# Edge blocks of a graph network: segment sums in bf16 over rows split into three parts by VectorE

## The reference

```python
def _ln(x, g, b): ...                        # layer norm over 64 features
def _mlp(x, w0, b0, w1, b1):
    return jax.nn.silu(x @ w0 + b0) @ w1 + b1
...
for s in range(S):                           # S = 2 blocks
    ce = jnp.concatenate([e, n[senders], n[receivers]], axis=-1)
    e = e + _ln(_mlp(ce, edge_blk_w0[s], edge_blk_b0[s], edge_blk_w1[s], edge_blk_b1[s]), ...)
    agg = jax.ops.segment_sum(e.astype(jnp.float32), receivers, num_segments=num_nodes)
    cn = jnp.concatenate([n, agg.astype(n.dtype)], axis=-1)
    n = n + _ln(_mlp(cn, node_blk_w0[s], ...), ...)
return _mlp(n, dec_w0, dec_b0, dec_w1, dec_b1)
```

## Time and profile before

| | us |
|---|---|
| median of 3 runs | 22607.06 (22599.68 to 22610.77) |
| the profiled execution's own time | 22640.54 |
| its span, first to last instruction | 22638.8 |
| POOL busy | 11698.9 |
| PE busy | 13646.0 |
| DVE busy | 9714.0 |
| ACT busy | 2931.8 |
| indirect DMAs of s0 and s1 (L804), issue time | 6148.6 |

### The profile page before, as it was taken

The page is one execution under the profiler, slowest core; times in us unless marked ns, Lnnn a source line. Parts: engine busy times, 40 slices in busy tenths (PEclk is TensorE's granted clock), DMA queues, the critical chain, the costliest instruction groups (busy, mean ns, idle before and its releaser), DMA issues. The chain is left out here.

```text
span 22638.8 us, 317898 instructions
## 1 busy us (share of the span) xinstructions
PE 13646.0 (60%) x88696; PEld 10718.9 (47%) x88696; DVE 9714.0 (43%) x29825; ACT 2931.8 (13%) x5120; POOL 11698.9 (52%) x12296
## 2 busy tenths in 40 slices
PE   2555555554787777845655555555456666666664
PEld 1444444443677677734444444444334444444443
DVE  4333333333666666643333333333343333333333
ACT  0222222221000000011111111111111111111111
POOL 5656565565444444444444444444445555555553
PEclk7666666565899899966666666666666666666666
DMA  2111111112111001113333333333323333333331
GB/s 86 54 55 55 55 55 54 56 54 58 20 21 21 20 20 21 21 44 102 102 101 102 102 101 102 102 102 101 88 78 93 92 93 92 93 92 93 91 92 53
DMA packets 1995040, 1603.29 MB, mean 71 GB/s; under 512 B 1291419, under 2 KB 1461007, under 8 KB 1994047
## 3 DMA queue, kind: packets, MB, share of 16 engines
q10 hardware_dynamic: 939256, 906.14, 12.2%
q0 software_dynamic: 394560, 282.16, 6.6%
q1 hardware_dynamic: 661104, 413.62, 6.5%
HBM read 990.92 MB, written 612.64 MB: 71 GB/s over the span
## 5 line engine op out<-in xcount | busy, mean ns | idle before, releaser
L804 POOL DMA_INDIRECT s_gt<-ta_d,s_ix x6448 | 6148.6, 954 | 5990.0 <-DVE s_ix L857 3804.4
L804 POOL DMA_INDIRECT g_gt<-xs_d,g_ix x3224 | 3047.6, 945 | 2084.4 <-DVE g_ix L857 1069.4
L1001 PE MATMUL pair<-g_part,g_Oh 128*128 128x224 bf16 x25389 | 2994.4, 276 | 750.9 <-issue 723.6
L1001 PEld LDWEIGHTS pair<-g_part,g_Oh 128*128 128x128 bf16 x25389 | 2531.5, 104 | 1123.4 <-issue 1001.4
L804 POOL DMA_INDIRECT g_gt<-ys_d,g_ix x2015 | 1921.1, 953 | 2124.8 <-DVE g_ix L857 1509.5
L1048 PEld LDWEIGHTS psw<-s_R,s_P 128*128 128x128 f32 x12896 | 2016.7, 228 | 2071.3 <-issue 2045.3
L1048 PE MATMUL psw<-s_R,s_P 128*128 128x64 f32 x12896 | 2001.9, 303 | 1421.6 <-issue 1392.9
L1015 PE MATMUL pair<-e_w,s_hT 128*128 128x128 f32 x6448 | 1350.9, 376 | 2240.6 <-ACT s_hT L953 1652.8
L1048 PE MATMUL psw<-g_R,g_P 128*128 128x80 f32 x6448 | 1250.3, 374 | 1831.2 <-ACT g_sg L958 1775.7
L1015 PEld LDWEIGHTS pair<-e_w,s_hT 128*128 128x128 f32 x6448 | 1195.0, 277 | 2385.4 <-ACT s_hT L953 1369.0
L1048 PEld LDWEIGHTS psw<-g_R,g_P 128*128 128x128 f32 x6448 | 1178.6, 282 | 2289.4 <-issue 2267.1
(11 more groups left out here) (329 smaller groups left out, 15662.6 us busy)
## 6 DMA issues: line engine op xcount, KB each, us to landing
s_dl<-dl_d SPq DMA_DIRECT2D x404, 512.0 KB
seg_d<-s_sg ACTq DMA_DIRECT2D x806, 256.0 KB
seg_d<-g_sg ACTq DMA_DIRECT2D x403, 320.0 KB
z_d<-g_rT ACTq DMA_DIRECT2D x403, 256.0 KB
s_z<-z_d ACTq DMA_DIRECT2D x403, 256.0 KB
s_gt<-ta_d,s_ix POOLq DMA_INDIRECT x6448
s_Bw<-tb_d ACTq DMA_DIRECT2D x3224, 32.0 KB
s_Bw<-tb_d SPq DMA_DIRECT2D x3224, 32.0 KB
```

Source lines behind the costliest of these rows:

```text
L804: eng.indirect_dma_start(out=gt[k][:, s, :], out_offset=None, in_=table[:, :], in_offset=bass.IndirectOffsetOnAxis(ap=ix[k][:, s:s + 1], a ...
L1001: last = eng.matmul(near_out(k, t), Oh[k][:, g, 128 * t:128 * t + 128], part[n][:, g, :, :].rearrange("p f l -> p (f l)"), start=g == 0 an ...
```

## The change

In s0 and s1 (and, as before, in g2) `cut` is now true. The one-hot `P` is bf16, and after writing the rows `R` DVE cuts them into three bf16 parts `Rp` whose sum is exactly the float32 value. PE's segment sums then take 24 bf16 matmuls (8 groups x 3 parts, accumulated in float32) where s0 and s1 had 8 float32 ones. DVE's scratch for the remainder is the square buffer `sq` of the same tile. A new semaphore, `v_cut`, says that the parts are there: PE waits for it before the segment sums, ACT before it overwrites `sq` two tiles later. In g2 the same four operations stay with another layout of `Rp`. The bias tables are three pieces of one tile at partitions 0, 32 and 64.

```diff
+        e_b1s = sbuf(ctx, "e_b1s", [67, 512], BF16)
+        e_b1 = [e_b1s[32 * i:32 * i + 3, :] for i in range(3)]
+        ones67 = sbuf(ctx, "ones67", [67, 128], BF16)
+        ones3 = ones67[0:3, :]
...
-                thin = near and not mlp
-                P = many("P", [128, G, 128], BF16 if thin else F32)
+                cut = expand or near and not mlp
+                P = many("P", [128, G, 128], BF16 if cut else F32)
+                if cut:
+                    Rp = many("Rp", [128, 3, G, FS], BF16)
...
+                if cut:
+                    rest = sq if mlp else many("rest", [128, G, FS])
...
+                    def parts_of(eng, k):
+
+                        eng.drain()
+                        eng.tensor_copy(Rp[k][:, 0, :, :], R[k][:, :, :])
+                        eng.drain()
+                        eng.tensor_tensor(rest[k][:, :, :], R[k][:, :, :], Rp[k][:, 0, :, :], ALU.subtract)
+                        eng.drain()
+                        eng.tensor_copy(Rp[k][:, 1, :, :], rest[k][:, :, :])
+                        eng.drain()
+                        return eng.tensor_tensor(Rp[k][:, 2, :, :], rest[k][:, :, :], Rp[k][:, 1, :, :], ALU.subtract)
...
                                 eng.tensor_tensor(R[k][:, :, 0:64], ps[2 + k][:, :].rearrange("p (s f) -> p s f", s=G),
                                                   bc(yy[:, :].rearrange("p (s o) -> p s o", o=1), [128, G, 64]),
                                                   ALU.mult).then_inc(v_ln.sem, 1)
+                                if cut:
+                                    parts_of(eng, k).then_inc(v_cut.sem, 1)
...
-                            done(eng, v_ln, j, L_LN + 2)
+                            done(eng, v_cut if cut else v_ln, j, L_LN + 2)
...
-                            eng.matmul(ps[2 + k][:, :], ones3[:, :], mlp[1][:, :], start=False, stop=True,
+                            eng.matmul(ps[2 + k][:, :], ones67[32 * mlp[1]:32 * mlp[1] + 3, :], e_b1[mlp[1]], start=False, stop=True,
...
+                            if cut:
+                                done(eng, v_cut, j, L_SEG)
...
-                                for n in range(3 if thin else 1):
-                                    last = eng.matmul(psw[:, SP_ * t:SP_ * t + FS], P[k][:, s, :], Rp[k][:, s, n, :] if thin else R[k][:, s, :],
-                                                      start=n == 0, stop=n == 2 or not thin)
+                                for n in range(3 if cut else 1):
+                                    last = eng.matmul(psw[:, SP_ * t:SP_ * t + FS], P[k][:, s, :], Rp[k][:, n, s, :] if cut else R[k][:, s, :],
+                                                      start=n == 0, stop=n == 2 or not cut)
```

More of the change, by code:

```diff
@@ L112, in build @@
         e_w1 = [sbuf(ctx, f"e_w1_{i}", [128, 128]) for i in range(3)]
-        e_b1 = [sbuf(ctx, f"e_b1_{i}", [3, 512], BF16) for i in range(3)]
-        ones3 = sbuf(ctx, "ones3", [3, 128], BF16)
+        e_b1s = sbuf(ctx, "e_b1s", [67, 512], BF16)
+        e_b1 = [e_b1s[32 * i:32 * i + 3, :] for i in range(3)]
+        ones67 = sbuf(ctx, "ones67", [67, 128], BF16)
+        ones3 = ones67[0:3, :]
         e_w0 = sbuf(ctx, "e_w0", [16, 128])
@@ L294, in dve @@
                     eng.memset(ones[:, :], 1.0)
-                    eng.memset(ones3[:, :], 1.0)
+                    eng.memset(ones67[:, :], 1.0)
                     eng.memset(one2[:, :], 1.0)
@@ L691, in build @@
         v_pt, p_rt, a_rt, v_sum, a_zr = [mark(f"e_{n}") for n in ("vpt", "prt", "art", "vsum", "azr")]
-        p_u, v_red, v_tab = [mark(f"e_{n}") for n in ("pu", "vred", "vtab")]
+        p_u, v_red, v_tab, v_cut = [mark(f"e_{n}") for n in ("pu", "vred", "vtab", "vcut")]
         s_m = [ctx.enter_context(nc.semaphore(f"e_mark{b}")) for b in range(2)]
@@ L737, in edge_loop @@
                     own = sbuf(c, f"{tag}_sel", [128, xp, FG, GL])
-                    Rp = many("Rp", [128, G, 3, FG], BF16)
-                    rest = sbuf(c, f"{tag}_rest", [128, G, FG])
                 if zout is not None:
@@ L891, in step @@
                                 landed(eng, s_g, GA, i, b, L_LN)
[L892 to L898, removed]
+                                eng.tensor_tensor(R[k][:, :, FM:FS], gt[k8][:, :, :],
+                                                  bc(ew2[:, bass.ds((j - L_LN) * G, G)].rearrange("p (s o) -> p s o", o=1),
+                                                     [128, G, FG]), ALU.mult).then_inc(v_msg.sem, 1)
+                                if cut:
+                                    parts_of(eng, k).then_inc(v_cut.sem, 1)
                         if stage(j, 0) and ew2 is not None:
@@ L1039, in step @@
                             done(eng, v_p, j, L_SEG)
+                            if cut:
+                                done(eng, v_cut, j, L_SEG)
                             if mlp:
                                 done(eng, v_ln, j, L_SEG)
-                            if ew2 is not None:
+                            if ew2 is not None and not cut:
                                 done(eng, v_msg, j, L_SEG)
@@ L1071, in edge_loop @@
                 v_ix.passed(NIST + 3)
+                if cut:
+                    v_cut.passed(NIST)
                 for m in (a_h, p_pre, p_x, a_sq, v_ln) if mlp else ():
@@ L1242, in norm16 @@
             return eng.tensor_tensor(x[:, :, :], x[:, :, :], b16(st[2]), ALU.mult)
[L1244 removed]
+        edge_loop("g1", 16, xs_d, seg80_d, mlp=(e_w1[0], 0), attr=True, zout=z_d, ew2=ew, counted=0)
         def conv1():
@@ L1607, in build @@
         cg.close()
-        edge_loop("s0", 64, ta_d, seg64_d, mlp=(e_w1[1], e_b1[1]), expand=True, zsrc=z_d, zw=zw[0], zout=e_d, counted=1)
+        edge_loop("s0", 64, ta_d, seg64_d, mlp=(e_w1[1], 1), expand=True, zsrc=z_d, zw=zw[0], zout=e_d, counted=1)
         node_phase("n0", seg64_d, nb_w0[0], n_b0[1], 1, edges=1, nxt=1)
-        edge_loop("s1", 64, ta_d, seg64_d, mlp=(e_w1[2], e_b1[2]), expand=True, zsrc=e_d, zw=zw[1], counted=2)
+        edge_loop("s1", 64, ta_d, seg64_d, mlp=(e_w1[2], 2), expand=True, zsrc=e_d, zw=zw[1], counted=2)
         node_phase("n1", seg64_d, nb_w0[1], n_b0[2], 2, edges=2)
```

6 lines of the change are left out of this document (removed).

## The result

The changed kernel takes 22794.45 us, median of 4 runs (22761.2 to 22802.61); before took 22603.37 on the same chip in 4 runs (22556.64 to 22610.77). The ratio is 1.0086, 95% interval 1.0071 to 1.0100: slower by 191 us. Forecast were 22990 and slower.

The account below looks back on a forecast made before the run. POOL's gathers plus delays of DVE's index copy were taken to bound s0 and s1. Terms 299 + 100 - 20 = +379 us on 22607 gave 22990 us; own range 22,830 to 23,150, with rivals 22,450 to 23,390.

Parts of the forecast that it names:

- The split's length: On DVE in s0 and s1, two casts and two subtractions add 2.51 us per step, between 2.1 and 3.1.
- +299 in s1: In s1, 117 POOL restarts have the 2.51 us split on their path, 294 us, and 8 more add 5.
- the first rival: Costly s1 restarts turn into the shorter-waiting kind, each saving 4.68 us; with 80 turned, 22410 us; chance 20%.
- +100 from the gathers: In s0 and s1, POOL's gathers that meet a DVE cast take 0.093 us longer, +100 us in all.
- The rival by which a cast stops the gathers wholly: In s0 and s1, gathers stand still for each whole cast: 448 us in place of 100, total 23330; chance 10%.
- -20 from PE: Segment sums of s0 and s1 get 0.7 us shorter per step, saving 20 us in both stages, bounds -116 and 0.
- s0 within 80: Stage s0 stays as long as before within 80 us, the split falling into idle time ahead of `s_rT` at restarts.
- The second rival: In s0, PE's sums wait for the parts, delaying copy, store, `s_rT` and `s_ix`: +394 us, total 23380; chance 12%.

Follow-up runs that it names:

- split_unused: Kernel before plus the split's four DVE operations in s0 and s1, result unread, float32 sums, shared bias tile: 22710.86 us, ratio 0.9985.
- g2_layout: Kernel before with only g2's three parts laid out as in the changed kernel: 22748.09 us, ratio 0.9992.
- no_split: Changed kernel without the split in s0 and s1: parts are zeros set once, the 24 bf16 matmuls a step stay: 22957.98 us, ratio 1.0076.
- rt_behind_ix: Kernel before with s0's `s_rT` moved on DVE to right behind `s_ix` of the same step, second kind of chip: 16151.08 us, ratio 0.9985.
- two_parts: Changed kernel with s0 and s1 summing two of the three parts, the third still made, second kind of chip: 16168.08 us, ratio 0.9996.
- after_again: Changed kernel, unaltered, run on a chip of the second kind: 16144.77 us, ratio 0.9995 to before.
- extra_passes: Kernel before plus one three-row bf16 matmul ahead of each slot's sum in s0 and s1, second kind of chip: 16504.28 us, ratio 1.0208.
- extra_f32: Kernel before plus 4 float32 matmuls a step in s0 and s1, at every second slot, second kind of chip: 16177.71 us, ratio 1.0001.

## Why the prediction came out as it did

The sign and the range held, but not for the reasons given. The kernels with one half of the change each say so: the split, for which the forecast had 299 + 100 = 399 us, measured -33 us alone (-80 to +14), and the sums, for which it had -20, measured +214 (89 to 257).

- **The split's length.** Forecast 2.51 us, from 0.693, 0.415 and 0.073. Measured 0.694 + 0.692 + 0.445 + 0.428 = 2.26 and (70.2 + 79.9 + 77.6 + 65.0) / 806 = 0.36 of idle time: 2.62 us. Right.
- **+299 in s1.** This is the step that failed: "In s1 the 117 restarts have the split between `s_R` and `s_Pt`, on the path". It took each restart of before as given and added 2.51 to it. split_unused shows the split alone: s1 5649 us, against 5708 in g2_layout, whose s1 is that of before; POOL's gaps of over 1.3 us 1577 against 1657. Restarts after more than 7 us fell from 93 to 51 there, shorter ones rose from 180 to 293. The fall is what the first rival said would come, and so is the direction. Its price was too high: it left the new short restarts out. A pair that ends in 9.2 us and turns into two single steps has two gaps of 4.6, and saves nothing; with 80 of 117 restarts turned the rival has s1 80 x 4.68 - 37 x 2.51 = 281 us shorter, and 59 were measured.
- **+100 from the gathers.** Their busy time rose by 6207.5 - 6148.6 = 59 us. ("Issue" in the same rows rose by 54, but that is the restarts which the view puts down to it; the gaps under 1.3 us fell from 1906 to 1888.) That the 59 are the split's work is shown by split_unused (mean gather 965 ns) beside no_split (953, with the same bf16 sums as the change). The price per gather was near and its bearer partly wrong: 472 gathers that began under a cast took 1.008 us on the mean and 1.14 at most, 498 that began under one of the two subtractions, to which the working gave nothing, 1.031, and those that met no DVE instruction at all 0.946. The rival by which a cast stops the gathers wholly is out. The Trainium skill (SBUF — State Buffer, section "SBUF: two separate sides") has GpSimd locked out for as long as such a copy runs. By it the term would have been 448 us, by the prediction's estimate; 59 were measured, an eighth, so the trace doesn't bear out a stop of the whole length for these gathers. As a cost of the kernel the term didn't show in split_unused. On the chips of the second kind there was no effect of the split on the mean (966 ns in rt_behind_ix without it, 966 in two_parts with it).
- **-20 from PE.** "What it gives PE" was seen rightly as a gain in length, and too small: 0.7 us a step forecast, and the sums of s0 fell from 3.5 to 2.2 us on the mean and those of s1 from 5.8 to 3.2. As a term it had the wrong sign. no_split, with such shorter sums, is slower by 0.76%; its s0 and s1 are 135 and 162 us longer than in g2_layout, in a profiled execution 73 us over its median. The working asked only who waits for the sums, and never whether earlier sums could move POOL's batches into another pattern.
- **s0 within 80.** It was +101, of which 97 are lost one-step batches and slightly dearer pairs. The second rival (PE waits for the parts, so copy, store and `s_rT` come later) had s0 paying 394 us. PE's 109 waits for the parts in s0 are real, but no_split has no such wait and its s0 is no shorter (6355), so this is not the cause.
- **The total.** That it fell into the range is luck: a term of 299 us that didn't come, and over 200 us from the bf16 sums that weren't in the sum. The two halves add up to -33 + 214 = 181 us, beside the 191 measured on another chip.

**What stays open.** That the bf16 sums cost the time is shown, on chips of the first kind; why is not. Ruled out for s0 are their number (8, 24 and 24 give 6334, 6345 and 6355 us, on three chips), a longer time of the sums (they are shorter), the split, the shared bias tile (it is in split_unused), g2's layout, and the writing of the one-hot on DVE, 1.22 us in either type. In no_split the parts are zeros besides, but s0 is as long with real ones. What is left is that sums in bf16, or the one-hot matrix in bf16, shift PE's work against POOL's batches so that the short restarts of s0 don't form, or that the new tiles move others in SBUF. A kernel with sums in bf16 that last as long as the float32 ones would test the shift; it wasn't run, and neither was `s_rT` behind `s_ix` on a chip of the first kind. Why s1 of the changed kernel has 20 gaps of 16 us behind three steps, and why its length with two parts lies between the others, is open too.

## What to carry to other kernels

Where one engine runs in batches and the others catch up in the gaps, a cost per restart is no constant: added work moves the kernel into another pattern of batches. So measure each half of such a change alone, and count the batches and their price per step before and after, since one sum of waits hides the trade: in s1 fewer long gaps stood against more short ones. And sum the gaps themselves: the wait row for `s_ix` fell by 29 us in s1 while all gaps grew by 70. A change that makes the work of an engine shorter that isn't the bound can cost time, as the 214 us of no_split show, whatever the way. And time a close call on more than one chip: what cost 0.86% on one kind was not to be measured on the other.

## What the runs showed of the hardware

**Two kinds of chips.** The same kernel takes 22.6 to 22.8 ms on one kind and 16.2 on the other. The gathers last as long on both (954 and 966 ns on the mean), and so do DVE's operations (`s_P` 1.22 us, `s_R` 0.69 on both). What differs is how SP, ACT and PE issue while POOL's gathers run, and the mean granted clock, 0.688 in the changed kernel's trace on the chip of the result against 0.779 in after_again. Eight issues of `s_Bw` in a row on SP, in the changed kernel on the chip of the result and then in after_again (start, us, instruction):

```profile
12998.20 10.39 SPq L762 DMA_DIRECT2D s_Bw<-tb_d  x8
```

```profile
13001.70 4.86 SPq L762 DMA_DIRECT2D s_Bw<-tb_d  x8
```

On the first kind instructions then often start 0.70 or 1.40 us apart. Of SP's gaps between two starts 5511 of 17777 have such a length in the trace of before, 5285 us in all; in after_again 58 of 17777 have, 42 us. DVE and POOL themselves are not slowed. On the second kind POOL never restarts in before's or the change's form of the loops: s0 and s1 have no gap of over 1.3 us and last about 403 x 10.1 us (only s1 of extra_passes has such gaps, 70 of them). So the waits from which the whole prediction was made exist on one kind of chip alone. What makes issue slow there, no run here shows.

**A small bf16 matmul between float32 ones on PE.** With a three-row bf16 matmul ahead of each float32 sum the groups took (extra_passes; count, busy, mean ns):

```profile
L1050 PE MATMUL psw<-s_R,s_P 128*128 128x64 f32 x12896 | 3236.6, 338 | 0.0
L1048 PE MATMUL psw<-e_b,ones 3*128 3x64 bf16 x6448 | 1321.8, 205 | 6.7 <-DVE s_R L913 3.4 <-issue 2.5 <-ACT s_sg L958 0.8
```

With a float32 matmul in its place at every second slot (extra_f32), as many recorded operations:

```profile
L1050 PE MATMUL psw<-s_R,s_P 128*128 128x64 f32 x12896 | 2153.6, 281 | 78.4 <-issue 65.5 <-DVE s_R L913 12.5
L1048 PE MATMUL psw<-s_R,s_P 128*128 128x64 f32 x6448 | 1301.1, 285 | 0.0
```

The windows of s0 and s1 in extra_f32, the columns of the earlier trace rows:

```profile
7480.00:11538.00 4058.00, 3237.15 (x23333) 2604.32 (x23334) 2413.88 (x7217) 692.83 (x1190) 3082.58 (x3180) 0.87 0.55 154
11820.00:15838.00 4018.00, 3152.58 (x21642) 2500.22 (x21642) 2183.67 (x6764) 694.45 (x1180) 3055.36 (x3158) 0.82 0.49 129
```

The three-row bf16 matmuls take 1322 us, and the float32 ones 1083 more than in extra_f32. PE's busy time in s1 is 4351 us of 4374, against 3153 in a window of 4018. The kernel is 2% longer, nearly all of it in s1 (4375 us from the first to the last copy of indices, against 4062); s0, with PE busy all the time too, took 4091 against 4078. The granted clock was lower, 0.67 in s1 and 0.79 in s0 (windows of extra_passes above), against 0.82 and 0.87, and the float32 matmuls took 364 ns in s1 and 312 in s0. How much of this is the changing type, how much the three rows and how much the clock isn't shown. The 24 bf16 matmuls in a row of the change did nothing like it on such a chip: in after_again PE is busy 2603 us of 4058 in s0.
